# Making the low parts of the attention weights on VectorE alone, on one Trainium2 core

## The reference

```
qt, kt, vt = (logmap0(q), logmap0(k), logmap0(v))
scores = jnp.einsum('bhqd,bhkd->bhqk', qt, kt) / math.sqrt(HD)
attn = jax.nn.softmax(scores, axis=-1)
out_h = expmap0(jnp.einsum('bhqk,bhkd->bhqd', attn, vt))
...
x = x + _L0_cond_ref(x, cond_1024[:, None, :], ...)
x = x + _L1_cond_ref(x, cond_1024, L1_cond_Wx, L1_cond_Wh, L1_cond_b)
```

## Time and profile before

| | |
|---|---|
| median of 3 runs | 1904.62 us (1903.64 to 1904.72) |
| the profiled execution's own time | 1905.15 us |
| its span in the profile | 1903.0 us |
| TensorE busy (matmul) | 1214.6 us, 64% |
| VectorE busy | 1174.1 us, 62% |
| ScalarE busy | 950.6 us, 50% |
| GpSimd busy | 404.2 us, 21% |

### The profile page before, as it was taken

How to read it: one execution, slowest core, us unless ns; L and a number is a source line. 1 busy time by engine, 2 the same in 40 slices (tenths; PEclk the granted TensorE clock), 3 DMA queues, 4 the chain that set the end, 5 groups by cost and what they waited for, 6 DMA issues and landing times.

```text
span 1903.0 us, 60748 instructions
## 1 busy us (share of the span) xinstructions
PE 1214.6 (64%) x21103; PEld 978.4 (51%) x21103; DVE 1174.1 (62%) x6657; ACT 950.6 (50%) x3287; POOL 404.2 (21%) x802
## 2 busy tenths in 40 slices
PE   4666677176777558867775588677764976444444
PEld 3544445145655445656554466555553665444443
DVE  6456634222777765657777666577776665666665
ACT  0333378234766644556666445466654554333332
POOL 4222234432221131311221312112114130000000
PEclk9667655588555557975555589655555886555555
DMA  8000000000000000000000000000000000000000
GB/s 257 0 0 0 0 1 0 1 1 1 3 0 0 2 3 2 2 25 3 0 1 3 2 2 2 25 2 0 1 2 3 2 2 13 0 0 0 0 0 13
DMA packets 14555, 17.85 MB, mean 9 GB/s; under 512 B 3348, under 2 KB 13208, under 8 KB 14360
## 3 DMA queue, kind: packets, MB, share of 16 engines
q1 hardware_dynamic: 10248, 10.50, 1.7%
q10 hardware_dynamic: 4112, 4.86, 0.9%
HBM read 13.25 MB, written 2.10 MB: 8 GB/s over the span
## 4 chain that ended last, share of the span: by engine, by line
PE 41%; DVE 25%; ACT 14%; issue 11%; POOL 6%; DMA 1%; POOLq 1%; ACTq 1%; DVEq 1%; SPq 0%
PE psum L727 20%; DVE cnew L1275 4%; DVE cadd L1272 4%; ACT tC L973 4%; DVE h L1283 3%; PE psum L701 3%; DVE h L1286 3%; PE psum L710 3%; DVE gO L1269 3%; PE psum L669 3%; POOL sc L226 3%; PE psum L679 2%; PE psum L559 2%; PE psum L596 2%; DVE h L1284 1%
## 5 line engine op out<-in xcount | busy, mean ns | idle before, releaser
L727 PE MATMUL psum<-h,wh 128*128 128x8 f16 x16384 | 514.6, 168 | 437.6 <-DVE h L1286 419.6
L727 PEld LDWEIGHTS psum<-h,wh 128*128 128x128 f16 x16384 | 479.7, 103 | 558.4 <-DVE h L1286 526.1
L967 ACT ACTIVATE tA<-gA 128x16 f32<-128x16 f32 x512 | 110.5, 216 | 474.5 <-DVE gA L1265 473.7
L1265 DVE TENSOR_REDUCE gA<-psum 128x16 f32<-128x32 f32 x512 | 97.4, 190 | 214.2 <-PE psum L727 213.5
L973 ACT ACTIVATE tC<-cnew 128x8 f32<-128x8 f32 x512 | 108.8, 213 | 130.9 <-DVE cnew L1275 87.3
L596 PE MATMUL psum<-qbd,kT 128*128 128x256 f16 x512 | 151.0, 400 | 24.5 <-ACT weights L853 21.5
L1272 DVE SCALAR_TENSOR_TENSOR cadd<-tA 128x8 f32<-128x8 f32 x512 | 126.8, 248 | 52.6 <-ACT tA L967 45.4
L853 ACT ACTIVATE weights<-psum 128x512 f16<-128x512 f32 x256 | 152.1, 594 | 0.0
L1283 DVE TENSOR_TENSOR h<-oU,tC 128x8 f16<-128x8 f32 x512 | 89.2, 174 | 97.1 <-ACT tC L973 96.3
L342 POOL TENSOR_TENSOR weights<-tmp,weights 128x512 f16<-128x512 f32 x64 | 74.0, 1157 | 313.2 <-ACT weights L853 313.2
L611 PEld LDWEIGHTS psum<-vs,weights 128*128 128x128 f16 x2048 | 112.3, 111 | 37.6 <-issue 17.2
(11 more groups left out here) (225 smaller groups left out, 2183.7 us busy)
## 6 DMA issues: line engine op xcount, KB each, us to landing
arena<-in_x_dram SPq DMA_DIRECT2D x4, 512.0 KB, 10.0
wf<-in_L_cond_w_f_dram SPq DMA_DIRECT2D x2, 1024.0 KB, 19.7
xs<-in_x_dram SPq DMA_DIRECT2D x4, 512.0 KB, 5.4
out_dram<-place SPq DMA_DIRECT2D x16, 128.0 KB, 2.1
arena<-in_L_cond_w_ada_dram ACTq DMA_DIRECT2D x1, 1536.0 KB
weights<-in_L_cond_Wh_dram ACTq DMA_DIRECT2D x1, 1024.0 KB, 14.7
gates<-in_L_cond_b_ada_dram ACTq DMA_DIRECT2D x8, 128.0 KB, 15.0
wx<-in_L_cond_Wx_dram SPq DMA_DIRECT2D x1, 1024.0 KB, 21.5
```

The costliest lines, as they stand in the source:

```text
L727: last = mm(cols, wh16[:, half, kc, (g0 + g) * P:(g0 + g + 1) * P], h16[:, kc, :, :], start=False, stop=g == n - 1 and kc == KD - 1 and ha ...
```

## The change

GpSimd's loop over the low parts goes, with the two signals that started its count. VectorE makes the low part of half 0 in slot 2hp+2 and that of half 1 in slot 2hp+3, each behind its step, and signals `t_l0` or `t_l1`. It gives the two starting signals of `t_l0` as well. Each still waits for the exps of its own half, which ScalarE made in the slot before. What is computed is unchanged, and so is what TensorE and ScalarE run.

```diff
@@ -452,11 +452,6 @@
 
                 n = j + 1
                 ch.round(n)
-                with pool.Fori(0, B * HP // 2) as i:
-                    for odd in range(2):
-                        hold(pool, "t_e0", B * HP * j + 2 * i + odd + 2)
-                        low_weights(g, odd, 0).then_inc(s["t_l0"], 1)
-
                 hold(pool, "t_rh", n)
                 rh, fr = num("rh", B * H), num("fr", B * H)
                 ch.link(g.tensor_scalar(fr, rh, REACH, 1.0, ALU.mult, ALU.min))
@@ -504,7 +499,6 @@
                 ch.full()
 
             hold(pool, "p_hk", NT)
-            pool.sem_inc(s["t_l0"], 2)
             ch = Chain(pool, s["achain"], s["held"], BLOCK_LINKS)
             pool_block(ch, 0)
             with pool.Fori(1, NB) as j:
@@ -1179,10 +1173,10 @@
                 last.then_inc(s["t_q"], 1)
 
             def dve_attention(k, b, q):
-                if q % 2 == 1 and 1 <= q // 2 <= HP:
-                    hp = q // 2 - 1
-                    v.wait_ge(s["t_e1"], HP * k + hp + 2)
-                    low_weights(d, hp % 2, 1).then_inc(s["t_l1"], 1)
+                if 1 <= q // 2 <= HP:
+                    hp, half = q // 2 - 1, q % 2
+                    v.wait_ge(s[f"t_e{half}"], HP * k + hp + 2)
+                    low_weights(d, hp % 2, half).then_inc(s[f"t_l{half}"], 1)
                 if q == LEAD:
                     v.wait_ge(s["t_qT"], k + 1)
                     q_twice((k + 1) % NT)
@@ -1348,6 +1342,7 @@
             v.wait_ge(s["p_kT"], NT + 1)
             q_twice(0)
             v.sem_inc(s["t_o"], 2)
+            v.sem_inc(s["t_l0"], 2)
             v.sem_inc(s["t_l1"], 2)
             v.sem_inc(s["t_r4"], 1)
             whole(0, None)
```

## The result

The changed kernel takes 1872.2 us (median of 4 runs, 1870.92 to 1874.7); the kernel before, run beside it, takes 1904.13. The ratio is 0.9834, with a 95% interval of 0.9817 to 0.9851. The forecast was 1872.6 with a range of 1865 to 1883.

The account below looks back on a forecast made before the run. Blocks 1 to 3 were taken as bound by LSTM step count times step length, with no engine full. Slot terms of -31.0 us and block 0's 1.0 gave 1873.15 from 1905.15, then 1872.6 as median; range 1865 to 1883.

Parts of the forecast that it names:

- The cause of the long slots: LSTM steps beside attention: GpSimd's low part holds VectorE's two-input L1272, 0.72 us instead of 0.16, lengthening 2.35 to 2.89.
- Slots 6, 8, 10: Attention with steps, 36 slots in all: 2.89 us becomes 2.36 without the stall, 19.1 us less.
- slot 2: Attention with steps: 1.6 us less in first batches; 7.5 less in the other 9, with 0.10 each for late TensorE.
- slot 3: Attention with steps, 9 times: normalization's last instruction L1204 falls from 1.15 us to 0.29 without GpSimd's stall, 7.7 us less.
- Slot 4: Attention with steps: copies of q fill the gap, so the low part costs 0.55 us; 5.0 more in 9 slots.
- Slot 11: Attention with steps, 12 times: the preceding copy of q blocks makes the tanh late, lengthening the slot by 0.25 us.
- Slot 14: Attention with steps, 12 times: stall of 0.53 us goes, low part beside the normalization costs 0.62; 1.1 us more.
- Block 0: Attention without steps: between 5 us gained and 1 us lost, taken as 1.0 us gained from fewer TensorE waits.
- TensorE in the place of the stall: Slots with sums: TensorE's matmuls use up the 0.24 us to spare, 10 us of gain go; 1882.6 us, chance 0.08.
- The clock: Attention with steps: denser TensorE work raises its clock, steps take 2.31 us instead of 2.35; 1864.6 us, chance 0.04.
- VectorE as the bound in every slot: Even slots: the low part does not fit beside the step's matmuls, 0.62 us each; 1918 us, chance 0.04.
- The stall not GpSimd's: L1272's 0.72 us has another cause, so only 14 us of low-part costs remain; 1918.7 us, chance 0.04.

Follow-up runs that it names:

- the second profile: The changed kernel run once more with nothing edited, to get another profile: 1873.37 us, ratio 0.9829 against the kernel before.

## Why the prediction was right

**The cause of the long slots.** Right. L1272 read as held by GpSimd's instruction: shown by taking the instruction out (47 us), by putting another one in its place (back, and more) and by one that reads nothing (not held).

**Slots 6, 8, 10; slot 2; slot 3.** 2.35 for 2.36, 2.47 for 2.46, 3.42 for 3.44. TensorE is late in slot 2, as read from where its matmuls ended. Slots 2 to 4 after, which answer to the earlier trace rows:

```profile
515.08 0.19 DVE L1259 TENSOR_REDUCE gA<-psum 128x16 f32<-128x32 f32 x1
...
516.50 0.60 PE L590 MATMUL psum<-qbd,kT 128*128 128x256 f16 x2
...
516.90 1.04 PE L721 MATMUL psum<-h,wh 128*128 128x8 f16 x32
...
517.55 0.19 DVE L1259 TENSOR_REDUCE gA<-psum 128x16 f32<-128x32 f32 x1
...
520.15 0.29 DVE L1198 TENSOR_TENSOR place<-place,sc 128x128 f32 x1
...
520.97 0.18 DVE L1259 TENSOR_REDUCE gA<-psum 128x16 f32<-128x32 f32 x1
...
522.65 0.69 DVE L342 TENSOR_TENSOR weights<-fT,weights 128x512 f16<-128x512 f32 x1
523.27 0.49 DVE L1172 COPY words<-qhl 128x512 f16 x2
523.67 0.18 DVE L1259 TENSOR_REDUCE gA<-psum 128x16 f32<-128x32 f32 x1
```

**Slot 4** was charged 0.55 and cost 0.41, under the lower bound of 0.51. The copies end at 523.76, but the gate sum starts at 523.67, before their end. It and slot 5 (2.29, the 0.06 that a late start gives back) came 2.4 us cheaper in all.

**Slot 11** was charged 0.25 us, 3.0 in all, for a tanh that would come late behind the copy of q blocks. The step failed. ScalarE in slots 10 to 12 after:

```profile
536.38 0.21 ACT L967 ACTIVATE tC<-cnew 128x8 f32<-128x8 f32 x1
536.50 0.58 ACT L847 ACTIVATE tmp<-psum 128x512 f32<-128x512 f32 x1
...
537.45 0.58 ACT L836 ACTIVATE qbd<-psum 64x512 f16<-64x512 f16 x1
537.98 0.22 ACT L961 ACTIVATE tA<-gA 128x16 f32<-128x16 f32 x1
...
538.90 0.60 ACT L847 ACTIVATE fT<-psum 128x512 f32<-128x512 f32 x1
...
540.01 0.59 ACT L836 ACTIVATE qbd<-psum 64x512 f16<-64x512 f16 x1
540.63 0.22 ACT L961 ACTIVATE tA<-gA 128x16 f32<-128x16 f32 x1
```

In slot 10 the copy starts 0.95 us after the first exp and ends at 538.03. The next tanh starts at 537.98, 0.22 behind its gate sum, as usual. In slot 11 the copy starts 1.11 us after the first exp. I had carried slot 11's lateness over to slot 10, though the kernel before had both distances already (541.00 to 541.96 and 543.40 to 544.51). Only the copy of slot 11 makes the next slot late (2.59).

**Slot 14** was mis-sized the other way: 3.40 for 3.39 in most, but 3.72 in the first batch of a block. Its end there:

```profile
505.00 0.68 DVE L342 TENSOR_TENSOR weights<-tmp,weights 128x512 f16<-128x512 f32 x1
...
506.00 0.29 DVE L1196 TENSOR_TENSOR place<-psum,place 128x128 f32<-128x128 f32 x1
506.80 0.29 DVE L1198 TENSOR_TENSOR place<-place,sc 128x128 f32 x1 [0.51 <-DVE place L1196]
507.01 0.18 DVE L1259 TENSOR_REDUCE gA<-psum 128x16 f32<-128x32 f32 x1
```

VectorE idles 0.51 us, though the inputs of the instruction behind are there. It is late in a like way in slot 7 of the first batch (2.64; 3.07 instead of 2.94 with both low parts in it), in every run with 256 low parts on VectorE and in none with fewer. That both come only in the first pass of the loop's body speaks for the supply of instructions, which no run here tests: it stays open.

**Attention in sum:** -35.1 us for -31.0 forecast; slots 11, 4 and 5 make 5.5 of the difference, slots 7 and 14 take back 2.3, and 1 us is spread over the others.

**Block 0** was to gain 1.0 us and gained nothing. TensorE's waits for low parts were 3.3 us again, in 5 places, and the time to the first step was 0.6 more, 0.0 in the second profile. From its first exp to its last sum block 0's attention took 86.4 us in the one and 86.2 in the other, against 85.4 before. But the two variants that differ from the changed kernel only in the order of VectorE's pieces took 84.8 and 84.6, so a term of 1 us cannot be read there in either direction.

**What was left out.** The rest of the blocks was held to be untouched, and gained 4.3 us. Of these, 1.0 is fixed: slots 91 and 102 of the 128 took some 0.16 us longer, three times each, in every profile with 256 low parts on VectorE and in none with fewer. One of them:

```profile
743.81 0.21 DVE L1269 TENSOR_TENSOR_SCAN cnew<-cmul,cadd 128x24 f32<-128x24 f32 x1
744.20 0.17 DVE L1272 TENSOR_SCALAR oU<-tO 128x8 f32<-128x8 f32 x1 [0.18 <-issue]
```

Of the remainder the slots that differ most are those with long float32 matmuls, and the one that was followed up (slot 103) moves with the clock. It does not move quite at random, though: it was long in 9 of 18 cases in the six profiles with 256 low parts on VectorE, and in none of 9 in the three with fewer. So the change may well cost something here by where the clock drops. How it would do that, no run shows. The hit within 0.4 us is partly luck: attention gained 4 us more than forecast, and the rest lost 4.

**The rivals.** TensorE in the place of the stall: no, it idled 0.24 us as read. The clock: 0.50 in attention as before. VectorE as the bound in every slot: no, though the margin was as thin as feared, and the run with both low parts in one slot shows its price: 0.59 us a slot. The stall not GpSimd's: no, as said first.

## What to carry to other kernels

GpSimd's work is not free because GpSimd is idle: ask which VectorE instructions run at that moment, and look in the timeline for one that takes several times its usual time and ends with GpSimd's. On the recurrence, VectorE can carry such work itself at no cost if each piece is the only one beside a matmul group that VectorE waits for anyway; of two pieces of 0.68 us in the same gap, the second cost 0.59. Forecast such a change by walking the slots of one period in the timeline, with a price for each, and look for gaps that other stages leave: the normalization moved into one gave 11 to 13 us more.

## What the runs showed of the hardware that I had not expected

- A fill on GpSimd that reads nothing held up a VectorE `tensor_scalar` of 128x8 (0.69 us instead of 0.17), while a two-input `scalar_tensor_tensor` ran beside it in 0.16.
- Three gate sums of VectorE on PSUM take 0.2 us apart when each comes just behind its matmuls, and 0.1 apart when they are late: 0.06 us of a delay is given back.
- The place at which TensorE's clock drops for a moment moves between runs of one kernel, and with it 1.6 us of a single group of eight float32 matmuls.
